# A two-hop graph kernel: the first hop gathers two more blocks of edges in place of their dense products

## What is computed

```python
deg  = segment_sum(ones, col) + 1          # every node has a loop to itself
dinv = rsqrt(deg)
for _ in range(2):                          # K_HOPS = 2
    h = segment_sum(h[row] * (dinv[row] * dinv[col])[:, None], col, N)
y = layernorm(x + log_softmax(h @ W.T + b))
```

## Time and profile before

| what | us |
| --- | --- |
| median of 3 runs | 2581.27 (2574.13 to 2583.68) |
| the profiled execution's own time | 2576.43 |
| its span, first to last instruction | 2574.0 |
| first hop, first to last add of a gathered group | 1678.2 to 2137.0 |
| first gather of the second hop starts | 2175.26 |
| last gather of the second hop starts | 2539.7 |

### The profile page before, as it was taken

One profiled execution on the slowest core, in us unless ns is written; L12 is line 12 of the kernel. 1 busy time (PEld: TensorE's weight loads), 2 busy tenths in 40 slices (PEclk: granted clock), 3 DMA queues, 4 the chain that ended last, 5 costly groups with the idle time before them and its releaser, 6 DMA issues.

```text
span 2574.0 us, 51283 instructions
## 1 busy us (share of the span) xinstructions
PE 2337.3 (91%) x16049; PEld 1834.0 (71%) x16049; DVE 2104.1 (82%) x5174; ACT 1490.0 (58%) x2727; POOL 1650.2 (64%) x1581
## 2 busy tenths in 40 slices
PE   7889999999999999999999996588999999999973
PEld 3369999999999999898988886134555554555542
DVE  6658888888889988989889999899898884456664
ACT  1157777777777777676767776354476671012232
POOL 0277777777777777676767763255565672777773
PEclk9989999999999999999999998799999999999996
DMA  6455555555555555555655553244545645676652
GB/s 214 177 188 171 168 167 169 172 170 170 166 168 165 168 167 178 166 163 164 179 162 169 174 163 95 90 115 120 154 131 153 158 116 166 235 237 228 206 155 87
DMA packets 276292, 422.47 MB, mean 164 GB/s; under 512 B 127634, under 2 KB 198692, under 8 KB 274004
## 3 DMA queue, kind: packets, MB, share of 16 engines
q0 software_dynamic: 90368, 281.11, 36.7%
q1 hardware_dynamic: 170028, 116.99, 15.5%
q10 hardware_dynamic: 15656, 21.30, 2.4%
HBM read 354.91 MB, written 64.37 MB: 163 GB/s over the span
## 4 chain that ended last, share of the span: by engine, by line
PE 51%; DVE 19%; issue 8%; ACT 8%; POOL 7%; DMA 5%; DVEq 1%; ACTq 0%; SPq 0%; POOLq 0%
PE banks L966 14%; POOL gathered L791 7%; PE banks L1054 5%; PE banks L943 4%; PE banks L1080 3%; ACT hidden_hi L1290 3%; PE banks L850 3%; DVE codes L1993 2%; PE banks L940 2%; PE banks L1028 2%; PE banks L941 2%; PE banks L980 2%; PE banks L982 2%; PE banks L953 2%; PE banks L954 2%
## 5 line engine op out<-in xcount | busy, mean ns | idle before, releaser
L791 POOL DMA_INDIRECT gathered<-p_table,src_t x784 | 798.0, 1018 | 397.4 <-DVE gate L1772 209.6
L791 POOL DMA_INDIRECT gathered<-hop_table,src_t x576 | 581.2, 1009 | 369.4 <-issue 154.9
L966 PE MATMUL banks<-w_hi,hidden_hi 128*128 128x256 f32 x1568 | 460.6, 294 | 29.4 <-DVE hidden_lo L1761 29.1
L966 PE MATMUL banks<-w_hi,hidden_lo 128*128 128x256 f32 x1568 | 443.3, 283 | 0.0
L966 PE MATMUL banks<-w_lo,hidden_hi 128*128 128x256 f32 x1568 | 443.2, 283 | 0.0
L1426 ACT CAST counts<-banks 128x686 f32 (+3 forms) x382 | 295.4, 773 | 179.7 <-PE banks L1028 81.7
L1297 ACT CAST msg_hi<-room 128x512 fp32r<-128x512 f32 x392 | 241.8, 617 | 228.2 <-DVE room L1780 228.2
L1761 DVE SCALAR_TENSOR_TENSOR hidden_lo<-banks,hidden_hi 128x512 fp32r<-128x512 f32 x392 | 269.9, 689 | 87.8 <-ACT hidden_hi L1290 86.2
L966 PEld LDWEIGHTS banks<-w_hi,hidden_hi 128*128 128x128 f32 x1568 | 299.7, 191 | 40.0 <-DVE hidden_lo L1761 39.5
L1028 PE MATMUL banks<-codes,low_hot 128*128 128x343 f16 (+3 forms) x958 | 240.5, 331 | 79.4 <-DVE codes L1993 63.0
L1311 ACT ACTIVATE gate<-gate 128x512 f32<-128x512 f32 x392 | 240.9, 632 | 110.8 <-DVE gate L1772 110.8
(11 more groups left out here) (225 smaller groups left out, 5266.4 us busy)
## 6 DMA issues: line engine op xcount, KB each, us to landing
ea<-in_edge_attr SPq DMA_DIRECT2D x196, 128.0 KB, 3.6
counts_saved<-counts SPq DMA_DIRECT2D x16, 1568.0 KB, 9.7
ring<-counts_saved SPq DMA_DIRECT2D x16, 1568.0 KB, 7.8
gathered<-p_table,src_t POOLq DMA_INDIRECT x784, 3.8
p_table<-p_t ACTq DMA_DIRECT2D x48, 256.0 KB, 4.2
hop_table<-parts SPq DMA_DIRECT2D x12, 896.0 KB
gathered<-hop_table,src_t POOLq DMA_INDIRECT x576, 2.9
x_saved<-x_room SPq DMA_DIRECT2D x7, 896.0 KB, 5.7
```

The costliest lines, as they stand in the source:

```text
L791: pool.indirect_dma_start(out=rows[:, n % slots, j, :], out_offset=None, in_=table[:, :], in_offset=bass.IndirectOffsetOnAxis(ap=src_t[:, ...
L966: last = nc.tensor.matmul(banks[:, 4 + half, j % 2 * H:(j % 2 + 1) * H], lhs, rhs, start=False, stop=n == len(products) - 1, skip_group_ch ...
```

## The change

The first hop gathers from group 116 (`FIRST[0]`) instead of 124: 80 turns in place of 72 (`TURNS`). It multiplies 18 blocks (`NF`), not 20. The second hop stays as it was, so `counts` is still built for all 20 blocks. Groups 116 to 123 also hold edges of blocks below 18, which the products have already; masks made in the setup (`first_of_hop`, `next_of_hop`) leave those out. `TENSOR_TURN` falls from 650 to 580. The chunks' order becomes 0, 1, 3, 4, 5, 2, 6, and their lower parts are written from inside the turns where `lowered_at` allows it. SP's load of the last weights waits for the counts instead of the products.

```diff
-STEP_COST, SCATTER_COST, TENSOR_TURN, SCALAR_TURN = 21, 100, 650, 650
+STEP_COST, SCATTER_COST, TENSOR_TURN, SCALAR_TURN = 21, 100, 580, 650
...
-    entry_ends, step_ends = plan.turns(SPARSE)
+    NF = NM - 2
+    FIRST = [min(g for g in range(0, DENSE, 2) if plan.upper[TILES * (g + 2)] >= P * NF), DENSE]
+    TURNS = [NG - FIRST[0], SPARSE]
+    EXTRA = FIRST[1] - FIRST[0]
+    entry_ends, step_ends = plan.turns(TURNS[0])
...
-        in_turn = [c for c in range(NC) if c != MIXED] + [MIXED]
+        in_turn = [c for c in range(NC - 1) if c != MIXED] + [MIXED, NC - 1]
...
+        def lowered_at(c):
+            passed = min(t for t in range(TURNS[0]) if step_ends[t + 1] >= min(NF * NB, (NF - 1) * NB + CHUNK * max(
+                NC if d == MIXED else d + 1 for d in in_turn[:in_turn.index(c) + 1])))
+            built_by = min(t for t in range(TURNS[0]) if entry_ends[t + 1] == NE)
+            return max(passed, built_by) + 2
...
-            sp.wait_ge(S["h0_multiplied"], NM)
+            sp.wait_ge(S["evac_done"], NE)
             sp.wait_ge(S["w_l_stored"], 16)
...
-            for g in range(DENSE, NG):
-                gather(hop_table[0], hop_rows, HOP_SLOTS, DENSE, "h0_gathered", "h0_scattered", 1, g)
+            for g in range(FIRST[0], NG):
+                gather(hop_table[0], hop_rows, HOP_SLOTS, FIRST[0], "h0_gathered", "h0_scattered", 1, g)
...
-                elif m == NM - 1 and b % CHUNK == CHUNK - 1:
+                elif m == NF - 1 and b % CHUNK == CHUNK - 1:
                     last.then_inc(S["part_free"], 1)
...
-                for turn in range(SPARSE):
+                for turn in range(TURNS[k]):
...
-                if k == 0:
-                    for b in range(NB):
-                        multiply(NM - 2, b)
-                        multiply(NM - 1, b)
...
-                nc.vector.tensor_single_scalar(first_of_hop[:, :], first_row[:, DENSE:NG], 1.0 / UPPER, ALU.mult)
-                nc.vector.tensor_single_scalar(next_of_hop[:, :], next_row[:, DENSE:NG], 1.0 / UPPER, ALU.mult)
+                for row, takes, of in ((NF, first_of_hop, first_row), (NF - 1, next_of_hop, next_row)):
+                    then(nc.vector.tensor_single_scalar(takes[:, :], of[:, FIRST[0]:NG], 1.0 / UPPER, ALU.mult))
+                    by_group = takes[:, 0:EXTRA].rearrange("p (r s) -> p r s", s=2)
+                    bases = banks[:, 4, 0:2 * R].rearrange("p (s r) -> p r s", s=2)[:, FIRST[0] // 2:DENSE // 2, :]
+                    nc.vector.scalar_tensor_tensor(out=by_group, in0=bases, scalar=float(P * row), in1=by_group,
+                                                   op0=ALU.is_ge, op1=ALU.mult)
...
                     if k == 0:
-                        for c in range(MIXED + 1, NC - 1):
-                            if turn == complete[c] - DENSE:
+                        for c in range(MIXED, NC - 1):
+                            if turn == complete[c] - FIRST[0]:
                                 dve.wait_ge(S["h0_agg_added"], turn)
-                                for t in range(CHUNK * c, CHUNK * (c + 1)):
+                                for t in range(max(NF, CHUNK * c), CHUNK * (c + 1)):
                                     scale_row(t)
-                add_hop(k, SPARSE - 1)
+                        for c in in_turn[:-1]:
+                            if turn == lowered_at(c):
+                                lower_chunk(1, c)
+                add_hop(k, TURNS[k] - 1)
...
-                for c in in_turn[:-2]:
-                    lower_chunk(1, c)
-                for m in range(NM - 2, NM):
-                    add_dense(0, m)
-                dve.wait_ge(S["h0_dense_added"], NM)
-                for t in range(NM - 2, CHUNK * (MIXED + 1)):
-                    scale_row(t)
-                for c in in_turn[-2:]:
-                    lower_chunk(1, c)
+                for c in in_turn:
+                    if c == NC - 1 or lowered_at(c) >= TURNS[0]:
+                        lower_chunk(1, c)
```

More of the change, by code:

```diff
@@ L354, in gnn_kernel @@
         next_row = sb("next_row", [P, NG])
-        first_of_hop = sb("first_of_hop", [P, SPARSE])
-        next_of_hop = sb("next_of_hop", [P, SPARSE])
+        first_of_hop = sb("first_of_hop", [P, TURNS[0]])
+        next_of_hop = sb("next_of_hop", [P, TURNS[0]])
         agg = sb("agg", [P, NB + 1, HP])
@@ L498, in gnn_kernel @@
         MIXED = (NM - 1) // CHUNK
-        in_turn = [c for c in range(NC) if c != MIXED] + [MIXED]
-        assert MIXED * CHUNK <= NM - 2 and complete[MIXED] > DENSE >= complete[MIXED - 1]
+        in_turn = [c for c in range(NC - 1) if c != MIXED] + [MIXED, NC - 1]
+        assert MIXED * CHUNK <= NF < MIXED * CHUNK + CHUNK and complete[MIXED] > DENSE and complete[MIXED - 1] <= FIRST[0]
+        def lowered_at(c):
[3 more added lines that the diff above has]
+            return max(passed, built_by) + 2
         LAST = [2, 3, 0, 4, 1, 5, NC - 1]
@@ L1075, in multiply_late @@
                         if i < BLOCKS + 2:
-                            pe.wait_ge(S["h0_dense_added"], NM)
+                            pe.wait_ge(S["h0_dense_added"], NF)
                         else:
@@ L1149, in hop @@
                             scatter_hop(k, turn, place_in // 2)
-                if k == 0:
-                    for b in range(NB):
-                        multiply(NM - 2, b)
-                        multiply(NM - 1, b)
             def gather_far(k, g):
                 for j in range(TILES):
-                    n = TILES * (DENSE * k + g) + j
+                    n = TILES * (FIRST[0] * k + g) + j
                     pe.wait_ge(S["far_ready"], n + 1)
@@ L1174, in gather_far @@
                     add_block(NB - 1, False, True)
-                pe.wait_ge(S["far_copied"], TILES * (DENSE * k + g) + TILES)
+                pe.wait_ge(S["far_copied"], TILES * (FIRST[0] * k + g) + TILES)
             def scatter_everywhere(k, g, spread_by, rows_of):
@@ L1195, in hop_anywhere @@
                 pe.wait_ge(S[f"h{k}_part_ready"], NB)
-                with pe.Fori(0, DENSE) as g:
+                with pe.Fori(0, FIRST[k]) as g:
                     gather_far(k, g)
@@ L1204, in scatter_near @@
                     pe.wait_ge(S[f"h{k}_gathered{n}"], 16 * TILES * (i + 1))
-                    scatter_everywhere(k, DENSE + HOP_SLOTS * i + n, hot_half,
+                    scatter_everywhere(k, FIRST[k] + HOP_SLOTS * i + n, hot_half,
                                        lambda j: [hop_rows[:, n, j, H * half:H * (half + 1)] for half in range(2)])
                     pe.sem_inc(S[f"h{k}_scattered"], 1)
-                with pe.Fori(0, SPARSE // HOP_SLOTS) as i:
+                with pe.Fori(0, TURNS[k] // HOP_SLOTS) as i:
                     for n in range(HOP_SLOTS):
                         scatter_near(i, n)
-                for n in range(SPARSE % HOP_SLOTS):
-                    scatter_near(SPARSE // HOP_SLOTS, n)
+                for n in range(TURNS[k] % HOP_SLOTS):
+                    scatter_near(TURNS[k] // HOP_SLOTS, n)
                 if k == 1:
@@ L1398, in upper_hop_rows @@
                 else:
-                    act.wait_ge(S["h0_multiplied"], NM)
+                    act.wait_ge(S["h0_multiplied"], NF)
                 nc.scalar.activation(parts[:, tiles, 0:H], agg[:, tiles, 0:H], ACT.Copy, scale=UPPER).then_inc(
@@ L2044, in hot_hop @@
             def hot_hop(k, turn):
-                if turn >= SPARSE:
+                if turn >= TURNS[k]:
                     return
-                t = TILES * (DENSE + turn)
+                t = TILES * (FIRST[k] + turn)
                 wait_count(dve, S[f"h{k}_scattered"], turn - HOT_TURNS + 1)
@@ L2059, in add_hop @@
                     return
-                g = DENSE + turn
+                g, column_of = FIRST[k] + turn, FIRST[k] - FIRST[0] + turn
                 row = dve.value_load(base_row[0:1, g % 2, g // 2:g // 2 + 1], min_val=0, max_val=NB - 1)
@@ L2066, in add_hop @@
                     last = nc.vector.scalar_tensor_tensor(out=where, in0=banks[:, bank_of_turn(k, turn), 0:H],
-                                                          scalar=takes[:, turn:turn + 1], in1=where, op0=ALU.mult,
+                                                          scalar=takes[:, column_of:column_of + 1], in1=where, op0=ALU.mult,
                                                           op1=ALU.add)
@@ L2188, in hop @@
                     return
-                for m in range(ends[SPARSE - 1] // NB, NM - 2):
+                for m in range(ends[TURNS[0] - 1] // NB, NF):
                     add_dense(0, m)
@@ L2229, in gather_far @@
                     nc.vector.tensor_single_scalar(far_rows[:, j, :], banks[:, 4, 0:H], 1.0 / UPPER, ALU.mult).then_inc(S["far_copied"], 1)
-                dve.wait_ge(S["far_copied"], TILES * (DENSE * k + g) + TILES)
+                dve.wait_ge(S["far_copied"], TILES * (FIRST[0] * k + g) + TILES)
             def add_everywhere(k, g, spread_by, scale):
```

(4 more changed lines are left out.)

4 lines of the change are left out of this document (2 added, 2 removed).

## The result

The changed kernel takes 2589.5 us in the median of 7 runs (2587.98 to 2596.15), the kernel before 2581.27 in 7 runs beside it (2574.13 to 2584.56): ratio 1.0043 [1.0032, 1.0055]. Forecast were 2588 and "the same" as likeliest.

A forecast was written before the change was run, and what follows sets the result against it. DVE was taken to bound the early full turns, PE the middle, and the second hop's first gather the end. Terms +13.0 + 8.9 - 16.6 + 0.7 + 1.0 = +7.0 us gave a median of 2588, range 2569 to 2608.

The forecast's parts named there:

- Part 1: Early turns, up to the 133rd entry: smaller budget moves products from DVE-set full turns into PE-set light ones, +13.0 us.
- Part 2: Middle of the first hop: 49 turns instead of 44 for the same entries, 288.5 us in all, +8.9 us.
- So here DVE becomes the floor: Six-entry turns of the middle: PE's work falls to 5.58 us, DVE's stays at 5.82, so a turn takes 6.15 us.
- the sign: Middle, turns 26 to 56: 6.1 to 6.2 us each, with DVE busier than PE, would confirm the forecast.
- Rival A: Middle: turns keep their lengths because engines hand entries on to each other; +29.5 us there, 2609 in all; chance 0.20.
- Rival B: Middle: gathers stretched to 1.25 us set the pace, turns at least 6.2 us; +24.1 there, 2603 in all; chance 0.05.
- Rival C: Whole first hop: engines mesh without waits, middle -3.7 us; -13.6 in all, 2568; chance 0.13.
- Part 3: Tail, to the second hop's first gather: 98 products go, six lower parts precede late adds; 30.0 us against 46.6, -16.6.
- Part 4: Small terms: setup's extra instructions and waits 0.7 us, and a later PE start in the second hop 1 us.
- the term of 1 us: Second hop: PE starts its first turn 15 us after the first gather, was 9.1; 1 us, nothing to 6.
- the setup's 0.7 us: Setup: two more DVE instructions of about 0.2 us and two more waits, 0.7 us; nothing to 1.
- The rule against the change: VectorE and GpSimd lock each other out of a shared port, so denser DVE work stretches gathers; sum used 1.041 us.

The follow-up runs named there:

- e7: Changed kernel with the first hop's one-hot table made for one tile of four from turn 4 on (sums wrong): 2584.12 us, ratio 1.0013.
- e3: Kernel before, with only PE's budget changed to 580 in its first 26 turns (650 after): 2748.01 us, ratio 1.0047, second chip.
- e9: Changed kernel with ACT's copies of the counts from entry 133 on cut to 24 of 49 source blocks: 2762.66 us, ratio 1.0089, third chip.
- e8: Changed kernel with SP's loads of the last weights and bias moved behind the first three loads of kept counts: 2769.62 us, ratio 1.0114, third chip.
- e6: Changed kernel with the second hop's lower parts written for one block of seven in chunks 0 to 5 (numbers wrong): 2584.85 us, ratio 1.0020.
- e5: Changed kernel with all lower parts behind the last add, not in two packs ahead of the adds of turns 76 and 77: 2595.62 us, ratio 1.0058.
- e4: Changed kernel with every lower part one turn earlier (turns 75 and 76): 2764.07 us, ratio 1.0105, second chip.

## Why the prediction was right, and where it was not

**The total** was forecast at +7.0 and is +8.2 between the medians (1.0043). Between the two profiled executions it is +10.4 (2586.86 against 2576.43). The three large terms erred by -1.0, +4.0 and +2.1 us; from the first add to the second hop's first gather +5.3 was forecast and +10.0 measured. These pieces repeat within 0.5 us in both profiles of the changed kernel, while the time ahead of the first add differs by 8.3 us between them. So the 1 us by which +7.0 misses the medians flatters the sum: that it came so near is in part luck.

**Part 1** (+13.0, measured 12.0) holds with its mechanism. Full turns stayed at 7.94 us with fewer products in them; e7 shows that DVE sets them, and e3 that the layout alone costs this (15.6 us on the second chip), on a kernel with the old number of turns.

**Part 2** (+8.9, measured +12.9; its own terms, 288.5 less 279.7, give 8.8) is the step that failed, in size and in its reason. "So here DVE becomes the floor" is refuted by e7. PE stayed the fullest engine. The sum could have told: I took 5.58, 5.22 and 5.6 us of PE's work for the three kinds of turns, which is 26 x 5.58 + 17 x 5.22 + 6 x 5.6 = 267.4 us in all. That is less than the 268.1 us before, though entries and products are as many and five scatters (4.5 us) come on top. The term that was too small is the 5.22: it came from a mean over 17 turns, of which two (60 and 61 in the old layout) carry 6 and no products. With the prices that I had, a turn with five entries and 13 products is 0.9 + 5 x 0.35 + 13 x 0.217 = 5.47 us. Kept whole, PE's sum would have been 272.6; measured were 276.0. The remaining 3.4 us of PE's work I can't assign.

Where the time was missed is another place. Turns 57 to 74 took 100.0 us, and the forecast's turn lengths give 100.4 for them; PE is busy 98% there. Turns 26 to 56 took 192.6 us in place of 188.1. That is 6.21 us a turn, within the 6.1 to 6.2 that I had named as the sign, but not with DVE busier than PE. There PE waits 13.1 us for ACT's copies, in all of the middle 3.7 us more than before. That this hand-over sets the pace is what the waits say; of the edits, e7 rules DVE out, and e9 shortens copies with some gain, on a chip where other waits disturb it. On the first chip it was not tested by itself.

**Rival A** (turns keep their lengths) is wrong on the first chip, where a middle turn went from 6.36 to 5.97 us; six-entry turns took 6.21 us from 26 to 39 and 6.58 from 41 to 47, where 6.15 was forecast and 6.57 is A's. On the second chip it is nearly true: a turn took 317.6 / 44 = 7.22 us before and 347.4 / 49 = 7.09 after, so that five more turns cost 29.8 us, A's 29.5. The forecast as a time held on the first chip, where PE's signals come at once. **Rival B** is out: the gathers of the middle had a mean of 1.03 us, not 1.25, POOL waited 42.5 us for PE, and shorter gathers in e7 left the middle as long as it was. **Rival C** is out as well, since no engine's work fell.

**Part 3** (-16.6, measured -14.5): two packs of three, their places and PE's idle time as forecast, the last add over at T + 18.5 in place of 18.8. Mis-sized is one term, the last store: 5.0 us taken, 7.4 measured. The upper bound, 7.47 from the earlier trace rows, was the right row. I had put its length down to the store and the loads around it; e8 moves the loads away, and 6.9 us are left of 7.8. In e6 it takes 8.2 us, though no other chunk's store is near. e5 shows that the packs' place is right, e4 that nothing is won by moving them further forward.

**Part 4.** PE's first scatter of the second hop came 11.4 us after the first gather, not 15: the products ran at the lower clock for only about 3 us, and POOL waited for PE only 0.9 us in the whole second hop. The hop is 0.9 us longer, as the term of 1 us says, but that is luck: POOL had waited 1.2 us for PE before as well, so this is not where it comes from. For the setup's 0.7 us no run shows anything: the first add comes 0.15 us earlier in one profile of the changed kernel and 8.1 later in the other.

**The rule against the change.** Two gathers beside the first pack of lower parts took 2.56 and 1.63 us instead of 0.95 (timeline above). In e5, where no lower part runs beside them, the same two take 0.95 and 0.94, and in e6, where each lower part is a seventh as wide, 0.96 and 0.95: so it is the long DVE instructions that stretch them. This agrees with what the Trainium skill, "SBUF — State Buffer", section "Who interferes with whom", says of a shared port that VectorE or GpSimd holds for a whole instruction while the other waits. It cost nothing, since PE was waiting for DVE then anyway.

## What to carry to other kernels

A plan that deals work into turns fixes more than the order: a smaller budget per turn takes work out from under the engine that sets the early turns and adds turns later, and both cost more here than the 98 products' removal gave. When turns get thinner, keep the sum of each engine's work and add what every further turn brings, rather than re-pricing one turn; the sum shows which engine stays the floor. Take a turn's price from its parts and not from a mean that may hold odd turns. Measure such a change on more than one chip, if it leaves less slack between engines that hand work on to each other. And where two engines stop at the same moment, look for the semaphore that both wait for before taking either for the cause.

## What the runs showed of the hardware

- The change costs 1.0040 on one chip. On two others, where every kernel takes 6% longer, it was not run bare, but e4 and e8, whose edits move next to nothing, stand at 1.0105 and 1.0114. There signals that PE's matmuls give to other engines come late, by up to 2.7 us in the moment shown under e4, and ACT, DVE and POOL wait for them; on the first chip they come within 0.02 us. The Trainium skill, "Runtime: NRT & Kernel Launch", section "Instruction fetch mechanics", says that each engine's instruction memory is refilled in blocks of 256 instructions while it runs; whether these stops are late refills, of PE then, no run here shows.
- An idle time of PE of about 2.3 us in dense work was in most cases followed by some 3 us at the lower of its two levels (1.2 instead of 2.4 GHz), and a pair of products took 1.03 instead of 0.59 us. In the tail, where PE had eight matmuls between 2155 and 2168.6, the clock stayed at 0.50 from 2158 to 2173.
- A gather's issue on POOL, 0.95 us by itself, took 2.56 and 1.63 us beside DVE instructions of 2.0 us on 128x1792 elements, and 0.95 again when these were moved away (e5) or cut to a seventh (e6).
- A chunk's store of 0.9 MB, issued by SP with no other chunk's store near, took 6.9 (e8) to 7.8 us from the issue until POOL went on. Behind six others (e5) its transfer alone took 11.0 us, against 7.1.
